# Attention in groups of 512 queries instead of 256, the second product with the values stationary, values streamed from DRAM, and the gated block computed behind each group

## The reference, cut to what matters

```python
# x: (2, 4096, 256), all float32
qkv = x @ w_attn + b_attn
q, k, v = jnp.split(qkv, 3, axis=-1)
mask = jnp.where(jnp.tril(jnp.ones((Tv, Tv), dtype=jnp.bool_)), 0.0, -10000000000.0)
attn = jnp.einsum('btc,bsc->bts', q, k) / jnp.sqrt(jnp.float32(Cv)) + mask
attn = jax.nn.softmax(attn, axis=-1)
out = jnp.einsum('bts,bsc->btc', attn, v)
attn_out = out @ w_proj + b_proj
x = _layernorm(x + attn_out, axis=-1)
# the block: k = 3072 rows with the highest router score get gelu(x @ w_block)
scores = jnp.einsum('bld,d->bl', x, w_router)
_, top_idx = jax.lax.top_k(scores, k)
processed = jax.nn.gelu(jnp.einsum('bkd,de->bke', selected, w_block))
x = _layernorm(x + x.at[batch_idx, top_idx].set(processed), axis=-1)
```

## Time and profile before

| | us |
|---|---|
| three runs | 1098.96, 1101.54, 1103.67 |
| median | 1101.54 |
| span of the profiled execution | 1098.8 |
| PE busy in it | 994.0 (90%) |
| DVE busy | 870.1 (79%) |
| ACT busy | 655.3 (60%) |
| POOL busy | 497.3 (45%) |

### The profile page before, as it was taken

How to read it: one execution, slowest core, us unless ns; L and a number is a source line. 1 busy time by engine, 2 the same in 40 slices (tenths; PEclk the granted TensorE clock), 3 DMA queues, 4 the chain that set the end, 5 groups by cost and what they waited for, 6 DMA issues and landing times.

```text
span 1098.8 us, 22231 instructions
## 1 busy us (share of the span) xinstructions
PE 994.0 (90%) x7894; PEld 972.0 (88%) x7902; DVE 870.1 (79%) x1875; ACT 655.3 (60%) x1250; POOL 497.3 (45%) x785
## 2 busy tenths in 40 slices
PE   6989999999999999889887999999999999987850
PEld 4979999999999999889876999899999999987750
DVE  1698787788768678686998998889887886976786
ACT  1665666667557557575553675666766764746425
POOL 3664443333322204244766476655653432324682
PEclk8999999999999999999998899999999999999895
DMA  3111110000000000011111012211110000010404
GB/s 95 55 39 40 40 40 30 21 30 30 11 21 28 11 21 21 1 40 37 52 49 49 30 59 69 67 37 43 49 40 20 21 20 11 20 30 30 144 30 153
DMA packets 45919, 44.81 MB, mean 41 GB/s; under 512 B 3441, under 2 KB 45810, under 8 KB 45810
## 3 DMA queue, kind: packets, MB, share of 16 engines
q1 hardware_dynamic: 45810, 43.40, 12.5%
HBM read 26.61 MB, written 16.78 MB: 39 GB/s over the span
## 4 chain that ended last, share of the span: by engine, by line
PE 62%; DVE 15%; issue 9%; POOL 9%; ACT 4%; DMA 1%; DVEq 0%; another core or an unknown queue 0%; ACTq 0%; POOLq 0%; SPq 0%
PE sbank L540 34%; PE obank L836 9%; PE obank L838 8%; PE obank L837 8%; DVE ring L793 3%; DVE ring_lo L812 2%; DVE runmax L704 2%; ACT tail_x L1303 1%; PE misc L753 1%; POOL rstd L852 1%; DVE sqscr L936 1%; ACT xres L927 1%; POOL ring L1239 1%; POOL fin L852 1%; PE misc L732 1%
## 5 line engine op out<-in xcount | busy, mean ns | idle before, releaser
L836 PE MATMUL obank<-V_hi,parts 128*128 128x258 f32 x1056 | 308.7, 292 | 19.0 <-DVE ring_lo L812 14.1
L540 PE MATMUL sbank<-qT_hi,xT_hi 128*128 128x256 f32 x1088 | 312.4, 287 | 2.3 <-ACT ring L692 2.3
L540 PE MATMUL sbank<-qT_lo,xT_hi 128*128 128x256 f32 x1088 | 308.0, 283 | 0.0
L540 PE MATMUL sbank<-qT_hi,xT_lo 128*128 128x256 f32 x1088 | 307.9, 283 | 0.0
L838 PE MATMUL obank<-V_hi,ring_lo 128*128 128x258 f32 x1056 | 301.5, 285 | 0.0
L837 PE MATMUL obank<-V_lo,parts 128*128 128x256 f32 x1056 | 300.8, 285 | 0.0
L812 DVE TENSOR_TENSOR ring_lo<-ring,parts 128x512 fp32r<-128x512 f32 x272 | 211.3, 783 | 34.1 <-ACT parts L806 32.8
L793 DVE TENSOR_TENSOR ring<-ring,maxrow 128x512 f32<-128x512 f32 x272 | 198.4, 756 | 35.2 <-ACT maxrow L762 35.2
L836 PEld LDWEIGHTS obank<-V_hi,parts 128*128 128x128 f32 x1056 | 203.3, 193 | 24.1 <-ACT parts L806 11.8
L540 PEld LDWEIGHTS sbank<-qT_hi,xT_hi 128*128 128x128 f32 x1088 | 207.5, 191 | 3.4 <-ACT ring L692 2.9
L540 PEld LDWEIGHTS sbank<-qT_lo,xT_hi 128*128 128x128 f32 x1088 | 207.7, 191 | 0.6
(11 more groups left out here) (182 smaller groups left out, 1595.0 us busy)
## 6 DMA issues: line engine op xcount, KB each, us to landing
xraw<-xt SPq DMA_DIRECT2D x32, 256.0 KB, 2.7
xres<-x SPq DMA_DIRECT2D x32, 256.0 KB, 2.7
x_scratch<-xres SPq DMA_DIRECT2D x32, 256.0 KB, 2.1
ring<-x_scratch SPq DMA_DIRECT2D x16, 256.0 KB, 2.6
out<-ring SPq DMA_DIRECT2D x16, 256.0 KB, 2.2
tail_x<-x_scratch SPq DMA_DIRECT2D x16, 256.0 KB, 2.6
out<-tail_g SPq DMA_DIRECT2D x16, 256.0 KB, 2.2
ring<-w_attn_t SPq DMA_DIRECT2D x3, 256.0 KB, 2.8
```

Source lines behind the costliest of these rows:

```text
L540: mm = eng.matmul(o, lhs(lh, k), rhs(rh, k), start=first and n == 0, stop=last and n == len(todo) - 1)
L836: pe.matmul(o[:, 0:VW], hi_, vh, start=first, stop=False)
```

## The change

The program is rewritten around wider tiles. The main pieces:

- GQ is 512: 8 groups for each batch. A score tile is 128 keys by 512 queries (6 products of 512 columns; the diagonal tiles have 512, 384, 256 and 128). The ring has NR = 34 slots. The operations on it take two tiles at once (1024 elements), but for the four diagonal tiles and the copy out of PSUM.
- The row maximum comes back by four transposes of a broadcast column, and DVE subtracts it straight from PSUM (`mbank`).
- The low part of every second pair goes to POOL (LO_EVERY = 2), 56 in all.
- The second product has V stationary and the probabilities moving, 512 columns. Its result has channels on the partitions, so ACT copies it to SBUF and PE turns it back, eight transposes for each group. V no longer has 258 columns: from each channel the last one is subtracted, the last becomes the column of ones, and the layer norm takes the shift out.
- V is written to DRAM (`v_scratch`), and each tile of 128 keys (256 KB, high and low) is loaded again for each group that needs it, 288 loads into NV = 6 buffers. x1 goes to DRAM as before, and x1 + gelu as well (`y_scratch`).
- The block is computed for every row right behind its group, with the gelu table of ACT, in both batches. What is left for after the search is three coefficients for each row, the reload of x1 and y, one scaling, one addition and the store.

```diff
-GQ = 256
-NR = 20
-NPB = 4
+GQ = 512
+NR = 34
+NV = 6
+NPB = 3
+LO_EVERY = 2
...
-                for t in range(QT):
-                    keys = slice((QT * j + t) * P, (QT * j + t + 1) * P)
-                    mm = split3(pe, o[:, t], lambda h, k: xT[h][:, k, keys],
-                                lambda h, k: qT[h][:, G % 2, k], CC)
+                if n >= NSS:
+                    pe.wait_ge(a_copy, n - NSS + 1)
+                split3(pe, sbank[n % NSS][:, c0:], lambda h, k: xT[:, h, k, kt * P:(kt + 1) * P],
+                       lambda h, k: qT[:, G % 2, h, k, c0:], CC).then_inc(p_s, 1)
...
-                act.copy(maxrow[:, G % 2], mb_ps).then_inc(a_mb, 1)
+                for t in range(QT):
+                    mm = pe.transpose(mt_ps[:, t], mcol[:, 2, t:t + 1].broadcast_to([P, P]), ident[:, :])
...
-                dve.tensor_tensor(slot3(n), slot3(n), maxrow[:, G % 2, None, :].broadcast_to([P, QT, GQ]),
+                dve.tensor_tensor(slots(ns, c0), slots(ns, c0),
+                                  mbank[:, None, c0:].broadcast_to([P, len(ns), GQ - c0]),
                                   ALU.subtract).then_inc(v_z, 1)
...
+            if lo_on_pool[u]:
+                at("pool", "softmax lo", 1, lambda pool: lo(pool, g_lo))
+            else:
+                at("dve", "softmax lo", 2, lambda dve: lo(dve, v_lo))
...
+            def load(sp):
+                if n >= NV:
+                    sp.wait_ge(p_pv, n - NV + 1)
+                Gk = gid(b, kt // QT)
+                sp.wait_ge(st_v[kt // 2 % 2], 16 * (Gk + 1))
+                sp.dma_start(f32(vs[:, n % NV]).rearrange("p h c -> p (h c)"),
+                             v_dram[b, kt].rearrange("p h c -> p (h c)")).then_inc(ld_v[n % NV], 16)
...
-                        pe.matmul(o[:, 0:VW], hi_, vh, start=first, stop=False)
-                        pe.matmul(o[:, 0:C], hi_, vl, start=False, stop=False)
-                        mm = pe.matmul(o[:, 0:VW], lo_, vh, start=False, stop=last)
+                for c in range(CC):
+                    o = obank[c][:, c0:]
+                    vh, vl = (vs[:, n % NV, h, c * P:(c + 1) * P] for h in range(2))
+                    pe.matmul(o, vh, lo_, start=i == 0, stop=False)
+                    pe.matmul(o, vh, hi_, start=False, stop=False)
+                    mm = pe.matmul(o, vl, hi_, start=False, stop=last)
...
+                act.copy(ot_sb[:, c, :], obank[c][:, :]).then_inc(a_ot, 1)
...
+                for j in range(2):
+                    filled(act, ("ff", G, j))
+                    act.activation(yb[:, 2 * j:2 * j + 2].rearrange("p t c -> p (t c)"),
+                                   bank_of(("ff", G, j))[:, :], ACT.Gelu_apprx_tanh).then_inc(a_gelu, 1)
...
+                    sp.wait_ge(p_s, n_tiles)
+                    filled(sp, ("v", B * NG - 1, 1))
...
+                sp.dma_start(x1.rearrange("p t c -> p (t c)"), x1_dram[b, u]).then_inc(done, 16)
+                sp.dma_start(y.rearrange("p t c -> p (t c)"), y_dram[b, u]).then_inc(done, 16)
```

More of the change, by code:

```diff
@@ L196, in then_inc, with work @@
         self.incs.append((self.time, sem.name, by))
-    def work(self, out):
-        self.time += self.fixed + self.per_element * int(np.prod(out.shape[1:]))
+    def work(self, out, n=None):
+        self.time += self.fixed + self.per_element * int(np.prod((out if n is None else n).shape[1:]))
         return self
@@ L278, in merged @@
     free = {e: START_US for e in streams}
+    busy = {e: 0.0 for e in streams}
     place = {e: {n: 0 for n in s} for e, s in streams.items()}
     queue = {e: [] for e in streams}
+    times = {e: [] for e in streams}
     def ready(waits):
@@ L309, in merged @@
                     best = (e, pick)
+        if best is None:
+            raise RuntimeError(f"no operation can start: {place}")
         e, (when, _, n) = best
@@ L313, in merged @@
         free[e] = when + time
+        busy[e] += time
         queue[e].append(make)
+        times[e].append((when, time, n))
         for t, name, by in incs:
@@ new lines, in program @@
+    first_tile[len(groups)], first_unit[len(groups)] = len(tiles), len(units)
+    n_tiles = len(tiles)
+    lo_on_pool = [len(ns) == 2 and (u - first_unit[G] - QT) % LO_EVERY == LO_EVERY - 1 for u, (G, ns, _) in enumerate(units)]
+    lo_count = [lo_on_pool[:u + 1].count(lo_on_pool[u]) for u in range(len(units))]
+    tile_no = {(G, kt): n for n, (G, kt, _) in enumerate(tiles)}
+    start_col = lambda n: (tiles[n][2] or 0) * P
+    proj_fills = [f for G in range(len(groups)) for f in (("q", G, 0), ("q", G, 1), ("v", G, 0), ("v", G, 1))]
@@ L1331, in program @@
+            at("sp", "final store", 3, store)
+        for G in range(len(groups)):
+            project(G)
+            for n in range(first_tile[G], first_tile[G + 1]):
+                scores(n)
+            running(G)
+            row_max(G)
+            for u in range(first_unit[G], first_unit[G + 1]):
+                softmax(u)
+            for n in range(first_tile[G], first_tile[G + 1]):
+                values(n)
+            attention_out(G)
+            ffn(G)
         for b in range(B):
@@ L1343, in program @@
+        queue, times = merged(streams)
         srch[0] = pool_steps[0] = 0
+        REHEARSED.update(times)
         block = ctx.enter_context(nc.Block())
-        wq_t, wk_t, wv_t, wp, wb = (ring[:, n, :].rearrange("p (k c) -> p k c", k=CC) for n in range(5))
-        small = misc[:, 0:8]
+        small = mbank[:, 0:8]
         @block.sync
```

1351 lines of the change are left out of this document (569 added, 782 removed).

## The result

The changed kernel takes **1163.49 us** (median of 4 runs, 1161.70 to 1168.24), the kernel before 1102.30 in the same comparison (4 runs, 1098.96 to 1103.67). The ratio is 1.056, 95% interval 1.053 to 1.060: 5.6% slower, where the prediction had 4% faster and a range that ended at 1105. The profiled execution has a span of 1161.2 us.

The account below looks back on a forecast made before the run. PE was taken as the bound: 23.5 us to the first q, 877 - 8 of PE work, 93 of PE losses and 68 for the end gave 1053.5, so 1056 as median, range 1010 to 1105.

Parts of the forecast that it names:

- PE's losses: PE's waits and half clock, from the early part to the last group, summed to 93 us.
- early 22: PE's loss in the early part: 22 us against 17 before, since the chain is longer and DVE leads.
- Small boundaries: Boundaries between groups from group 3 on: 8 us lost, with 3 to 6 score tiles put into each chain.
- Change of batch: From group 7's products to group 4 of batch 1, DVE needs more time than PE: 35 us lost, 53 before.
- the last group: x1 and y loads queue ahead of V tiles: 7 us late, 4 of half clock, 8 of chain; 20 in the sum.
- the gelu's 8: A gelu pair with two table loads holds ACT and delays score copies at 14 places: 8 us of PE.
- The totals of the other engines: DVE busy 810 to 840 us, POOL waits of 60 to 90 included, and ACT 680; neither bounds the kernel.
- A wider product: A 512-column product on PE takes 0.2155 us, bounds 0.213 and 0.239; PE's work falls from 945 to 877, 68 us.
- The start: PE's first q at 23.5 us instead of 20.1, behind POOL's b_tot addition and low part of x.
- The end: From the last product with V to the finish, with search and final scaling: 68 us instead of 81.
- The rival of 38 us: Gelu holds the scores' copies in full, PE standing at ten of 14 places: 38 us, not 8; 1086, chance 0.08.
- POOL's low parts: Rival: low parts on POOL hold the products with V, +62 to +90 less what the 93 has; 1120, chance 0.12.

Follow-up runs that it names:

- c13: The changed kernel with only its order altered, by corrected estimates and the searched priorities: 1096.83 us, ratio 0.995.
- c10: c9 with the priorities of the changed kernel in place of the searched ones: 1118.82 us, ratio 1.014.
- c9: The changed kernel with corrected estimates, low parts all on DVE, 33 searched priorities, and start, last loads and final power reordered: 1043.85 us, ratio 0.948.
- c6: The changed kernel with batch 1's final x1 and y loads waiting for the 6th last product with V, not the last score tile: 1151.34 us, ratio 1.045.
- c2: The changed kernel in its own order with tanh in place of gelu in the block, leaving one table load of 28: 1160.53 us, ratio 1.053.
- c11: c9 with every second pair's low part on POOL again and POOL's interference in the estimates: 1075.97 us, ratio 0.976.
- c12: c9 without the loads of V after the sixth, later products taking old values: 1044.78 us, ratio 0.948.
- c5: The changed kernel in its own order, PE's part of the block taking constants so it skips waits for norm and split: 1159.09 us, ratio 1.051.

## Why the prediction was wrong, point by point

- **PE's losses (93 us): this step failed**, the measured sum is 163. Its terms: early 22, measured 19 up to 100 us. Small boundaries 8, measured 18 from 100 to 400, where the text itself had set 12 as the limit. Change of batch 35, measured 33 from 400 to 700. From 700 to the last product with V 93, where the prediction had only the last group (20) and some of the gelu's 8. What had no term in the sum is PE's waiting at the boundaries of batch 1. I had taken them to be like those of batch 0, with work in front of each chain. In that stretch the trace lists 67 us of waits in many kinds, 15 us are half clock, and the rest are short gaps. Counting what stands ahead of the turn of the normalised rows finds only one of these places before the last product with V (6 instructions, 8.2 us); the others would have needed every wait of the plan. I had read the order at two or three places, and I argued from engine totals ("DVE stays below PE"), which say nothing on an order fixed in advance. The last paragraph of the prediction named this risk without a chance for it. Of the 163, the replay has 108 in the plan itself, and another order takes back 63 (c13 loses 100).
- **The totals of the other engines: too high, and no help.** DVE is busy for 775 us (810 to 840 predicted), ACT for 625 (680). DVE's waits for POOL, taken as 60 to 90, are some 26 on its 84 wide maxima (1.397 where 1.22 was clean) and 56 wide low parts (1.414). With all engines below their predicted totals PE still waited more.
- **A wider product at 0.2155: mis-sized**, it is 0.2265, which the bounds 0.213 to 0.239 held. 3072 x 0.011 = 34 us. I read the f32 product L753 as a stand-in, and its records carry only 2 ns above the columns that I gave them; why they do is not shown. The rows of the fp32r product itself said 0.1195 against 0.107 for its columns, and the 13 ns in that are the fixed part at 256, 384 and 512 columns. The Trainium skill ("TensorE: Matmul & The Clock Gate", Back-to-back issue gap) has the column time plus 2.5 ns for a lone product, 0.216 here, and a sustained 0.131 for 512 columns; the trace agrees with neither. PE's whole work fell from 945 to 909, by 36 us and not by 68, so the change had only half the gain to lose.
- **The start: half right.** POOL's order was the mechanism (b_tot ahead of the low part of x), but b_tot itself came 4 us later than I had it:

```profile
21.91 2.37 POOL L726 TENSOR_TENSOR xres<-xres,b_tot 128x1024 f32<-128x1024 f32 x1 [11.62 <-DVE b_tot L1217]
24.25 2.78 POOL L432 TENSOR_TENSOR xT<-xraw,xT 128x1024 fp32r<-128x1024 f32 x1
```

  With the low part first, PE starts its first q at 18.3 in c10 instead of 27.1.
- **The end (68 us): right**, 67.8, though one piece that I had not priced is in it. DVE waits 5.7 us for POOL's power of 32 columns:

```profile
1134.27 5.43 POOL L701 TENSOR_TENSOR fin<-fin,half 128x32 f32<-128x32 f32 x1
...
1141.71 0.19 DVE L1028 SCALAR_TENSOR_TENSOR coef<-fin,sel 128x32 f32<-128x32 f32 x1 [5.70 <-POOL fin L1019]
```

  With 28 columns done early the end is 62.7 in c9 and c10.
- **The last group: right** in place, and near in size: 6.1 us of waiting (7 predicted), and 8.3 with the half clock by c6 in that group (7 + 4 predicted).
- **The gelu: 8 us predicted**, nothing that can be told from zero (c2). The rival of 38 us falls.
- **POOL's low parts: the rival was real, its size about half.** I priced it 64 us above the forecast, with a chance of 0.12; c11 has 32, part of which may be order. Its mechanism is shown for 5 us only, PE's waits that end with a low part of POOL; 10 us are longer operations of DVE, and the rest is open. The forecast had counted POOL's price only on DVE.
- **The stream of V: right**, hidden (c12).

Sum of the two that failed: 34 + 70 = 104 of the 107 us between 1056 and 1163. With its order mended and four small edits the changed kernel reaches 1044. That compares a searched order with one that was not: how much the kernel before would gain by such a search was not run.

## What to carry to other kernels

Where the order of every engine is fixed in advance, a rewrite is two changes, the work and the order, and the second can be larger than the first: here 75 us against 36 of work saved. Before judging such a change, replay the plan and read its planned waits; count at every boundary how much work stands in front of each long chain, of every kind and not of one; and set priorities again after tile sizes have changed, serving first what the bound engine waits for next and last what only runs ahead. A wait in the profile is worth what removing it brings. Here 13 us of waits at the end were worth nothing (c5), while one of 6.1 us in the last group was worth 8, with the half clock behind it (c6). And look in the trace whether an edit took the wait away: in c5 the bank kept half of it.

## What the runs showed of the hardware

- An fp32r product with its own weight load costs its columns at 2.4 GHz plus 13 ns, at 256, 384 and 512 columns; at half clock (1.2 GHz) exactly its columns (0.427 for 512, 0.213 for 256). At 128 columns it is 0.11 at full clock. Going from 256 to 512 columns is worth 12.5 ns for each wide product, 5%.
- POOL's power takes 1.02 us on four columns and 5.43 on 32 (means 1.08 and 5.50), so about 0.16 for each column, while a multiplication of the same 32 columns takes 0.25.
- Leaving out 27 of 28 table loads of 1.28 us on ACT (c2 against the changed kernel) changed nothing that can be measured, and so did leaving out 74 MB of DMA traffic beside the products (c12 against c9).
